# Row maxima of two heads in two 64-row tiles of the array, from the upper halves of the queries and keys

## The chip, the core and the metric

The kernel runs on one core of one Trainium2 chip. The core has a matrix engine (TensorE, here PE, its weight loads PEld), a vector engine (DVE), a scalar engine (ACT), GpSimd (POOL) and the queue of SyncE (SP), which issues the transfers. The metric is the device time of one execution in microseconds (us). Three executions took 2843.00, 2849.17 and 2850.83 us; the median is 2849.17.

## The reference

An image stack x of 4 x 128 x 32 x 32 goes through three layers: a non-local block, an attention layer over the 1024 tokens of each of 4 images, and a mixture of 8 experts, top 2. The change is in the attention layer. It has 16 heads of 64 (32 plain, 32 rotary) and three branches, each with its own keys and values:

```python
o1 = _attn(q, k1, v1, causal)            # all tokens, causal
o2 = _attn(q, ks, vs)                    # 256 selected tokens
o3 = _attn(q, kw, vw, winmask)           # causal, the last 64 tokens
o = g[:, 0] * o1 + g[:, 1] * o2 + g[:, 2] * o3
```

with `_attn` the softmax of `q k^T / 8` times v.

## The kernel before, in words

The program has three parts, one after the other: `heads_part` (non-local block, queries, keys and values of all heads, written to DRAM), `attention_part`, and `experts_part`. The attention part works by sides: a side is a pair of heads, so 8 sides to an image, 32 in all. `turns` is called three times: once to prepare the first side (OPENING), once as a loop over images 0 to 2 (MIDDLE), and once for image 3 (CLOSING).

Queries and keys are kept as an upper part (hi) and a rest (lo), in two sets of 128 rows. In the first set (q1a with k1a for branch 0, qa with kwa and ksa for branches 2 and 1) the upper 64 rows of a query tile are the hi parts of the head and the lower 64 its rests, and the keys have their hi parts twice, so that one matmul over 128 rows gives (hi + rest) of q times hi of k. The second set (q1b, qb, with k1b, kwb, ksb) adds hi of q times the rest of k, and in one row more the negated row maximum. The exponential thus comes straight out of PSUM.

In window w TensorE computes the exact pass of side w, and in between prepares side w+1, that is, finds the row maxima of its scores. The exact pass (`exact_pass`) has 25 units (branch, 512-column chunk of queries, 128-token tile of keys; 512 columns wide or fewer), each with `scores` (L1352, masks L1355 and L1358, L1360, for both heads), an exponential on ACT (L1409) and `products` (L1381, probabilities times values and, with a weight of ones, the sums; four column tiles of 32, fp32, in two passes). Two units' products follow every second unit's scores.

The preparation (`preparation`) is a list of fills, 43 to a side, in the order that TensorE, DVE and SP all follow: max2 (8 fills: head, pair of query tiles; the window), max1 (8; the selected), max0 (24; head, query tile, 512-column part; causal), three transposes ("rows") that turn the maxima into a row, and "whole", the last reduction of max0 (DVE). A fill of max0 is one matmul q1a x k1a (L1288), and where it reaches the diagonal a mask product with a bf16 identity (L1291). A fill of max1 has two products of 256 columns (L1299); one of max2 two of 192 (L1307), each with its mask (L1309). `window` spreads the list over the exact pass: after the scores of a unit it puts fills in until their share is that of the columns passed. Each fill takes one of three PSUM banks (SPARES) in turn; fill n waits until DVE has emptied fill n-3 (semaphore `emptied`), and DVE reduces each bank to its maxima (L1462, L1467).

SP issues the loads: `local` (qa, kwa, ksa and the second sets of branches 1 and 2; two sides ahead, L1206 to L1218), `whole` (q1a, k1a and the second set of branch 0; one side ahead, L1227 to L1232) and `row` (the maxima's row into row 64 of qb and q1b, L1239). Each transfer of queries fills 32 rows for both heads (`two`). `near`, `keys`, `far`, `late` count them.

Of the kernel before, what the change touches and what calls it, by code (L numbers as in the profile page):

```python
# [15 lines left out]
P = 128  # L16
B, C, T = 4, 128, 1024
NT = T // P
# [1040 lines left out]
class Plan:  # L1059


    def __init__(self, steps, sides, loads):
        self.steps, self.sides, self.loads = steps, sides, loads
        self.fills = self.of(("max0", "max1", "max2", "rows", "proj"))

    def of(self, kinds):
        return [x for x in self.steps if x[0] in kinds]

    def up_to(self, kind, side):

# [108 lines left out]
def turns(nc, m, plan, cur, nxt):  # L1179
# [7 lines left out]
                             "banks_free inverse_done divided o_done max_done")  # L1187
    negs = [m.small[:, k * HP * NT:(k + 1) * HP * NT] for k in range(3)]
    partial = m.small[:, 64:64 + HP * NT * 2].rearrange("p (h t a) -> p h t a", h=HP, t=NT)
    NEAR, KEYS, FAR, LATE = 8, 10, 5, 4  # L1190

    def two(x, side):

        return x[HP * NOPE * (side % 2):HP * NOPE * (side % 2 + 1)].rearrange("(h r) n -> r h n", h=HP)

    with nc.Block() as block:
        @block.sync
        def _(sp):
            def local(side):
                k, src = side % 2, cur if side < NSIDE else nxt  # L1200
                g, own = side % NSIDE // 2, side % NSIDE
                if side >= 2 and cur is not None:
                    sp.wait_ge(s["products_done"], len(UNITS) * (side - 2) + LOCAL)
                near, keys = s["near%d" % k], s["keys%d" % k]
                for at, comp in ((0, 2), (32, 4), (64, 3), (96, 5)):
                    sp.dma_start(m.qa[at:at + 32, k].bitcast(F32), two(src.q[g, comp], side)).then_inc(near, 16)  # L1206
                for at, comp in ((0, 0), (32, 2), (64, 0), (96, 2)):
                    sp.dma_start(m.kwa[at:at + 32, k].bitcast(F32), two(src.kw[g, comp], side)).then_inc(near, 16)
                for at, comp in ((0, 0), (32, 2), (64, 0), (96, 2)):
                    sp.dma_start(m.ksa[at:at + 32, k].bitcast(F32), two(src.ks[g, comp], side)).then_inc(keys, 16)  # L1210
                for at, comp in ((0, 2), (32, 4)):
                    sp.dma_start(m.qb[at:at + 32, k].bitcast(F32), two(src.q[g, comp], side)).then_inc(keys, 16)
                for at, comp in ((0, 1), (32, 3)):
                    sp.dma_start(m.kwb[at:at + 32, k].bitcast(F32), two(src.kw[g, comp], side)).then_inc(keys, 16)
                    sp.dma_start(m.ksb[at:at + 32, k].bitcast(F32), two(src.ks[g, comp], side)).then_inc(keys, 16)
                vv = slice(NW * own, NW * (own + 1))
                sp.dma_start(m.vw[:, k], src.vw[:, :, vv].rearrange("t p n -> p t n")).then_inc(s["late%d" % k], 16)
                sp.dma_start(m.vs[:, k], src.vs[:, :, vv].rearrange("t p n -> p t n")).then_inc(s["late%d" % k], 16)  # L1218

            def whole(side):  # L1220
# [5 lines left out]
                for at, comp in ((0, 0), (32, 4), (64, 1), (96, 5)):  # L1226
                    sp.dma_start(m.q1a[at:at + 32, k].bitcast(F32), two(src.q[g, comp], side)).then_inc(far, 16)  # L1227
# [42 lines left out]
        def _(pe):  # L1270
# [7 lines left out]

            def fill(n, kind, side, *a):

                if n >= SPARES:
                    pe.wait_ge(s["emptied"], n - SPARES + 1)
                bank, k = ps[:, 8 - SPARES + n % SPARES, :], side % 2
                if kind == "max0":
                    h, i, part = a
                    once("far%d" % k, 16 * FAR * plan.loaded("whole", side))
                    k0, k1 = part * CH, min((part + 1) * CH, (i + 1) * P)
                    mm = pe.matmul(bank[:, 0:k1 - k0], m.q1a[:, k, h, i * P:(i + 1) * P],  # L1288
                                   m.k1a[:, k, k0:k1], start=True, stop=True)
                    if k1 == (i + 1) * P:  # L1290
                        mm = pe.matmul(bank[:, k1 - k0 - P:k1 - k0], m.ident_bf[:], m.causal_q[:],  # L1291
                                       start=False, stop=True, skip_group_check=True)
                elif kind == "max1":
                    h, pair = a
                    once("near%d" % k, 16 * NEAR * plan.loaded("local", side))
                    once("keys%d" % k, 16 * KEYS * plan.loaded("local", side))
                    for i in range(2):
                        t = 2 * pair + i
                        mm = pe.matmul(bank[:, i * KEEP:(i + 1) * KEEP], m.qa[:, k, h, t * P:(t + 1) * P],  # L1299
                                       m.ksa[:, k, h, :], start=True, stop=True)  # L1300
                elif kind == "max2":
                    h, pair = a
                    once("near%d" % k, 16 * NEAR * plan.loaded("local", side))
                    for i in range(2):
                        t = 2 * pair + i
                        k0 = max(0, t * P - WINDOW)
                        pe.matmul(bank[:, i * KEEP:i * KEEP + WN], m.qa[:, k, h, t * P:(t + 1) * P],  # L1307
                                  m.kwa[:, k, h, k0:k0 + WN], start=True, stop=True, skip_group_check=True)
                        mm = pe.matmul(bank[:, i * KEEP:i * KEEP + WN], m.ident_bf[:],  # L1309
                                       m.window_q0[:] if t == 0 else m.window_q[:], start=False, stop=True,  # L1310
                                       skip_group_check=True)
                elif kind == "rows":
                    if a[0] == 0:
                        pe.wait_ge(s["max_done"], plan.nth(side) + 1)
                    else:
                        pe.wait_ge(s["emptied"], plan.up_to(("max1", "max2")[a[0] - 1], side))
                    mm = pe.transpose(bank[0:HP * NT, 0:P], negs[a[0]], m.ident[:])
                elif kind == "proj":
                    c, g = a[0], side // 2
                    cc = slice(c * CH, (c + 1) * CH)  # L1320
                    pe.wait_ge(s["divided"], plan.count("divide", side, SUMS.index((0, c)), PIECES - 1))
                    pe.wait_ge(s["o_done"], PIECES * (NC * g + c + 1))
                    pe.matmul(bank, m.wvp[:, g], m.products[:, 0, cc], start=True, stop=False)
                    mm = pe.matmul(bank, m.wproj[:, g], m.products[:, 1, cc], start=False, stop=True)
                mm.then_inc(s["fill_ready"], 1)

            def scores(side, u):
                br, c, j, q0, w = UNITS[u]
# [57 lines left out]
            for step in plan.steps:  # L1386
                if step[0] == "scores":
                    scores(*step[1:])
                elif step[0] == "products":
                    products(*step[1:])  # L1390
                elif step in plan.fills:
                    fill(n, *step)
                    n += 1

        @block.scalar
        def _(act):
# [41 lines left out]
        def _(dve):  # L1438
# [3 lines left out]
            for step in plan.steps:  # L1442
# [14 lines left out]
                n += 1  # L1457
                dve.wait_ge(s["fill_ready"], n)
                if kind == "max0":
                    _, _, h, i, part = step  # L1460
                    w = min((part + 1) * CH, (i + 1) * P) - part * CH
                    ins = dve.tensor_reduce(partial[:, h, i, part:part + 1], bank[:, 0:w], AX, ALU.max)  # L1462
                elif kind in ("max1", "max2"):
                    _, _, h, pair = step
                    w = KEEP if kind == "max1" else WN
                    at = h * NT + 2 * pair
                    ins = dve.tensor_reduce(negs[1 if kind == "max1" else 2][:, at:at + 2],  # L1467
                                            bank.rearrange("p (i n) -> p i n", i=2)[:, :, 0:w], AX, ALU.max,
                                            negate=True)
                elif kind == "rows":  # L1470

                    br = step[2]
                    if plan.nth(side) > 0:
# [560 lines left out]
```

## Time and profile before

The profiled execution took 2847.5 us, its span is 2845.7 us, the mean granted clock of TensorE 0.898 of full speed.

| engine | busy us | share of the span | instructions |
|---|---|---|---|
| PE | 2338.5 | 82% | 16656 |
| PEld | 1554.8 | 55% | 16656 |
| DVE | 1629.2 | 57% | 3043 |
| ACT | 1265.5 | 44% | 2777 |
| POOL | 669.0 | 24% | 687 |

```profile
PE   5586868663999999899999799999899999610995
PEclk9696979775999999999999899999899999755997
DMA  2254645477556555556556465665475461431113
```

The span is cut into 40 slices of 71 us; a digit is the busy share of a slice in tenths. Slices 10 to 34 are the attention part. PE's digits count a matmul from its start to its modelled end, and matmuls overlap, so a 9 does not say how many columns passed. PEclk is the granted clock of TensorE in tenths of full speed.

### The profile page before, as it was taken

What the parts mean: (1) busy time and instruction counts of PE and PEld (TensorE: products, weight loads), DVE (VectorE), ACT (ScalarE), POOL (GpSimd) and SP (SyncE); (2) the same over time, 40 slices, a digit from 0 to 9 for tenths busy, and PEclk for the clock granted to TensorE, in tenths of its full rate; (3) what the DMA queues carried; (4) which work ended last, traced back from release to release, by engine and by line L of the source; (5) the groups of instructions that cost most, each with busy time, mean ns of one, the idle gap of its engine ahead of it and who ended that gap; (6) DMA issues with size and microseconds to landing.
All of it is one profiled execution on the core that took longest, in us unless ns stands there. A gap on an engine that the chain in (4) does not pass through costs nothing. (4 is left out here: it accounts for less than half of the span.)

```text
span 2845.7 us, 46717 instructions
## 1 busy us (share of the span) xinstructions
PE 2338.5 (82%) x16656; PEld 1554.8 (55%) x16656; DVE 1629.2 (57%) x3043; ACT 1265.5 (44%) x2777; POOL 669.0 (24%) x687
## 2 busy tenths in 40 slices
PE   5586868663999999899999799999899999610995
PEld 3454545442666665566666466666566666410884
DVE  4757575724566556366466365565465664450666
ACT  2354545440555554455555345555355555410442
POOL 0264646581011001011011010010010110135332
PEclk9696979775999999999999899999899999755997
DMA  2254645477556555556556465665475461431113
GB/s 94 102 226 163 231 163 229 162 288 166 124 117 129 117 124 113 119 114 133 123 108 139 91 129 111 129 131 103 105 146 126 96 140 37 132 55 51 47 51 108
DMA packets 222862, 360.73 MB, mean 127 GB/s; under 512 B 68794, under 2 KB 124701, under 8 KB 222240
## 3 DMA queue, kind: packets, MB, share of 16 engines
q1 hardware_dynamic: 218304, 349.20, 49.2%
q0 software_dynamic: 4320, 8.43, 0.9%
q8 instruction: 140, 2.29, 0.4%
q14 instruction: 98, 0.80, 0.1%
HBM read 229.58 MB, written 126.56 MB: 125 GB/s over the span
## 5 line engine op out<-in xcount | busy, mean ns | idle before, releaser
L1409 ACT ACTIVATE prob<-ps 128x512 f32<-128x512 f32 (+5 forms) x1600 | 637.3, 442 | 732.8 <-PE ps L1360 586.8
L1462 DVE TENSOR_REDUCE maxima<-ps 128x1 f32<-128x512 f32 (+3 forms) x768 | 387.7, 548 | 294.8 <-PE ps L1288 147.0
L1432 POOL TENSOR_TENSOR products<-products,sums 128x256 f32<-128x256 f32 x192 | 140.4, 731 | 1605.9 <-DVE sums L1453 1604.6
L1381 PE MATMUL ps<-prob,plain 128*32 128x512 f32 (+5 forms) x3200 | 512.0, 443 | 0.0
L1467 DVE TENSOR_REDUCE maxima<-ps 128x2 f32<-128x512 f32 (+1 forms) x512 | 294.4, 608 | 243.2 <-PE ps L1309 108.5
L1453 DVE RECIPROCAL sums<-sums 128x256 f32<-128x256 f32 x192 | 331.5, 1736 | 104.1 <-ACT sums L1420 104.1
L1352 PE MATMUL ps<-q1a_s,k1a_s 128*128 128x512 f32 (+3 forms) x768 | 303.2, 395 | 0.0
L1360 PE MATMUL ps<-q1b_s,k1b_s 128*128 128x512 f32 (+3 forms) x768 | 301.2, 393 | 0.0
L1381 PE MATMUL ps<-prob,v_s 128*32 128x512 f32 (+3 forms) x1536 | 284.3, 491 | 0.0
L1288 PE MATMUL ps<-k1a_s,q1a_s 128*128 128x512 f32 (+3 forms) x768 | 234.7, 375 | 3.4 <-DMA k1a_s<-k1ah_dram 3.4
L1418 ACT ACTIVATE products<-ps,gates_a 64x512 f32<-64x512 f32 x192 | 131.0, 683 | 195.1 <-PE ps L1381 195.0
L1352 PEld LDWEIGHTS ps<-q1a_s,k1a_s 128*128 128x128 f32 x768 | 147.1, 191 | 126.8 <-issue 119.0
L953 POOL TENSOR_TENSOR pairs<-pairs 128x512 fp32r<-128x512 f32 (+1 forms) x112 | 134.7, 1208 | 290.6 <-ACT pairs L921 290.5
L1352 PE MATMUL ps<-qa_s,kwa_s 128*128 128x192 f32 (+2 forms) x576 | 175.0, 304 | 19.7 <-ACT prob L1409 16.1
L1360 PE MATMUL ps<-qb_s,kwb_s 128*128 128x192 f32 (+2 forms) x576 | 184.1, 322 | 0.0
L1352 PEld LDWEIGHTS ps<-qa_s,kwa_s 128*128 128x128 f32 x576 | 109.8, 191 | 98.3 <-issue 65.6
L1288 PEld LDWEIGHTS ps<-k1a_s,q1a_s 128*128 128x128 f32 x768 | 145.5, 196 | 21.8 <-DVE maxima L1462 8.4
L1360 PEld LDWEIGHTS ps<-q1b_s,k1b_s 128*128 128x128 f32 x768 | 151.3, 197 | 5.5
L1307 PE MATMUL ps<-kwa_s,qa_s 128*128 128x192 f32 x512 | 125.3, 327 | 34.7 <-DMA kwa_s<-kwh_dram 34.7
L1381 PEld LDWEIGHTS ps<-prob,plain 128*32 128x32 f32 x3200 | 147.2, 109 | 0.0
L1352 PE MATMUL ps<-qa_s,ksa_s 128*128 128x512 f32 x256 | 114.1, 446 | 37.4 <-issue 19.3
L1358 PE MATMUL ps<-window_k,ident_bf 128*128 128x192 bf16 (+2 forms) x576 | 141.3, 245 | 0.0
(333 smaller groups left out, 4862.7 us busy)
## 6 DMA issues: line engine op xcount, KB each, us to landing
qh_dram<-pairs SPq DMA_DIRECT2D x96, 512.0 KB, 2.7
kwh_dram<-pairs SPq DMA_DIRECT2D x64, 512.0 KB, 2.7
qa_s<-qh_dram SPq DMA_DIRECT2D x128, 256.0 KB, 4.4
kwa_s<-kwh_dram SPq DMA_DIRECT2D x128, 256.0 KB, 7.4
q1a_s<-qh_dram SPq DMA_DIRECT2D x128, 256.0 KB, 4.7
qb_s<-qh_dram SPq DMA_DIRECT2D x64, 256.0 KB, 9.1
kwb_s<-kwh_dram SPq DMA_DIRECT2D x64, 256.0 KB, 10.0
k1a_s<-k1ah_dram SPq DMA_DIRECT2D x32, 512.0 KB, 6.9
```

The costliest lines, as they stand in the source:

```text
L953: pool.tensor_tensor(lo.bitcast(F32R), lo, hi.bitcast(F32), ALU.subtract)\
L1288: mm = pe.matmul(bank[:, 0:k1 - k0], m.q1a[:, k, h, i * P:(i + 1) * P], m.k1a[:, k, k0:k1], start=True, stop=True)
L1352: pe.matmul(bank, kx, qx[:, k, h, q0:q0 + w], start=True, stop=False, skip_group_check=True)
L1358: pe.matmul(bank, m.ident_bf[:], m.window_k[:, at:at + w], start=False, stop=False, skip_group_check=True)
L1360: pe.matmul(bank, ky, qy[:, k, h, q0:q0 + w], start=False, stop=True, skip_group_check=True)\
L1381: mm = pe.matmul(ps[at:at + VD, SCORES + k % 2, q0 - c * CH:q0 - c * CH + w], w_, m.prob[:, n % PROBS, h, 0:w], start=first, stop=True, sk ...
L1409: act.activation(m.prob[:, u % PROBS, h, 0:w], ps[:, turn % SCORES, 0:w], ACT.Exp, scale=SCALE).then_inc(s["exp_done"], 1)
L1418: act.activation(m.products[rows, br, cc], ps[0:NW, SCORES + k % 2, :], ACT.Copy, scale=m.gates[0:NW, br:br + 1])
L1432: pool.tensor_tensor(o, o, m.sums[:, br, cc], ALU.mult).then_inc(s["divided"], 1)
L1453: dve.reciprocal(total, total).then_inc(s["inverse_done"], 1)
L1462: ins = dve.tensor_reduce(partial[:, h, i, part:part + 1], bank[:, 0:w], AX, ALU.max)
L1467: ins = dve.tensor_reduce(negs[1 if kind == "max1" else 2][:, at:at + 2], bank.rearrange("p (i n) -> p i n", i=2)[:, :, 0:w], AX, ALU.max, ...
```

## The change

Both heads of a side are prepared by one step. Its matmuls use 64 rows each: head 0 rows 0 to 63, head 1 rows 64 to 127, both with hi of q and hi of k only, into two banks. For that the loads put head 1's hi parts into the lower 64 rows of q1a and qa and its rests into the upper 64 (`upper_and_lower`); the exact pass still multiplies all 128 rows and gets the same sum. The masks stay products of 128 rows, after both heads' matmuls. 40 fills become 20 steps of two banks each; a step waits for both banks before its first matmul. DVE reduces the two banks one after the other, as before. Queries of the first sets come in 8 transfers of one head each instead of 4 of both.

```diff
 def preparation(side):
-    max0 = [("max0", side, h, i, part) for h in range(HP) for i in range(NT) for part in range(1 + (i >= NT // 2))]
-    max1, max2 = [[(kind, side, h, k) for h in range(HP) for k in range(NT // 2)] for kind in ("max1", "max2")]
-    todo = max2 + max1[:3] + [("rows", side, 2)] + max1[3:] + max0[:3] + [("rows", side, 1)] + max0[3:]
+    max0 = [("max0", side, i, part) for i in range(NT) for part in range(1 + (i >= NT // 2))]
+    max1, max2 = [[(kind, side, k) for k in range(NT // 2)] for kind in ("max1", "max2")]
+    todo = max2 + max1[:2] + [("rows", side, 2)] + max1[2:] + max0[:2] + [("rows", side, 1)] + max0[2:]
     return todo + [("whole", side, 0)]
...
-    NEAR, KEYS, FAR, LATE = 8, 10, 5, 4
+    NEAR, KEYS, FAR, LATE = 12, 10, 9, 4
+    def one(x, side, h):
+        return x[HP * NOPE * (side % 2) + NOPE * h:HP * NOPE * (side % 2) + NOPE * (h + 1)]
+    def upper_and_lower(first):
+        return [(h, at, comp + (lo ^ h)) for h in range(HP) for lo in range(2)
+                for at, comp in ((64 * lo, first), (64 * lo + 32, 4))]
...
-                for at, comp in ((0, 2), (32, 4), (64, 3), (96, 5)):
-                    sp.dma_start(m.qa[at:at + 32, k].bitcast(F32), two(src.q[g, comp], side)).then_inc(near, 16)
+                for h, at, comp in upper_and_lower(2):
+                    sp.dma_start(m.qa[at:at + 32, k, h].bitcast(F32), one(src.q[g, comp], side, h)).then_inc(near, 16)
...
+                def bank(h):
+                    if n + h >= SPARES:
+                        pe.wait_ge(s["emptied"], n + h - SPARES + 1)
+                    return ps[:, 8 - SPARES + (n + h) % SPARES, :]
+                upper = [slice(HD * h, HD * h + HD) for h in range(HP)]
                 if kind == "max0":
+                    both = [bank(h) for h in range(HP)]
+                    last = [pe.matmul(both[h][:, 0:k1 - k0], m.q1a[r, k, h, i * P:(i + 1) * P], m.k1a[r, k, k0:k1],
+                                      start=True, stop=True, skip_group_check=True) for h, r in enumerate(upper)]
                     if k1 == (i + 1) * P:
+                        last = [pe.matmul(both[h][:, k1 - k0 - P:k1 - k0], m.ident_bf[:], m.causal_q[:],
+                                          start=False, stop=True, skip_group_check=True) for h in range(HP)]
+                    for mm in last:
+                        mm.then_inc(s["fill_ready"], 1)
                 elif kind == "max1":
+                    both = [bank(h) for h in range(HP)]
                     for i in range(2):
+                        for h, r in enumerate(upper):
+                            mm = pe.matmul(both[h][:, i * KEEP:(i + 1) * KEEP], m.qa[r, k, h, t * P:(t + 1) * P],
+                                           m.ksa[r, k, h, :], start=True, stop=True, skip_group_check=True)
+                            if i == 1:
+                                mm.then_inc(s["fill_ready"], 1)
                 elif kind == "max2":
+                    both = [bank(h) for h in range(HP)]
                     for i in range(2):
+                        for h, r in enumerate(upper):
+                            pe.matmul(both[h][:, i * KEEP:i * KEEP + WN], m.qa[r, k, h, t * P:(t + 1) * P],
+                                      m.kwa[r, k, h, k0:k0 + WN], start=True, stop=True, skip_group_check=True)
+                    for h in range(HP):
+                        for i in range(2):
+                            mm = pe.matmul(both[h][:, i * KEEP:i * KEEP + WN], m.ident_bf[:],
+                                           m.window_q0[:] if 2 * a[0] + i == 0 else m.window_q[:], start=False, stop=True,
+                                           skip_group_check=True)
+                        mm.then_inc(s["fill_ready"], 1)
...
-                bank = ps[:, 8 - SPARES + n % SPARES, :]
+                for h in range(plan.banks(step)):
+                    bank = ps[:, 8 - SPARES + n % SPARES, :]
+                    n += 1
+                    dve.wait_ge(s["fill_ready"], n)
...
```

## Rows read from the trace of the kernel before

**Rows 1.** Busy time by stretch, us; two neighbouring windows of one side.

```profile
core 0: us, PE busy (x) PEld busy (x) DVE busy (x) ACT busy (x) POOL busy (x), PEclk, DMA share, GB/s
...
1468.64:1521.35 52.71, 51.33 (x430) 32.60 (x429) 26.45 (x47) 27.51 (x63) 1.45 (x2) 1.00 0.59 123
1521.35:1574.27 52.92, 51.02 (x425) 31.90 (x423) 38.12 (x54) 27.52 (x63) 10.26 (x14) 1.00 0.59 122
```

**Rows 2.** Waits in these two windows: total us, times, longest.

```profile
ACT prob L1409 <- PE ps L1360: 37.7, 37, 4.9
...
PEld ps L1323 <- DVE maxima L1467: 1.8, 1, 1.8
...
PE ps L1352 <- ACT prob L1409: 0.9, 3, 0.4
```

**Rows 3.** Timeline of PE, causal fills (start us, length us, instruction).

```profile
1507.45 0.37 PE L1288 MATMUL ps<-k1a_s,q1a_s 128*128 128x256 f32 x1
...
1507.70 0.42 PE L1288 MATMUL ps<-k1a_s,q1a_s 128*128 128x384 f32 x1
...
1508.00 0.47 PE L1352 MATMUL ps<-q1a_s,k1a_s 128*128 128x512 f32 x1
```

**Rows 4.** Timeline of PE, two products of a max2 fill.

```profile
1468.77 0.33 PE L1307 MATMUL ps<-kwa_s,qa_s 128*128 128x192 f32 x1
...
1468.98 0.33 PE L1307 MATMUL ps<-kwa_s,qa_s 128*128 128x192 f32 x1
```

**Rows 5.** Timeline of all engines, max1 fills and their reduction.

```profile
1481.29 0.45 PE L1299 MATMUL ps<-ksa_s,qa_s 128*128 128x256 f32 x2
...
1481.77 0.69 DVE L1467 TENSOR_REDUCE maxima<-ps 128x2 f32<-128x512 f32 x1 [1.26 <-PE ps L1299]
...
1482.49 0.63 PE L1299 MATMUL ps<-ksa_s,qa_s 128*128 128x256 f32 x4
```

**Rows 6.** Timeline of PE, from column tiles back to the full array.

```profile
1501.19 0.39 PE L1381 MATMUL ps<-prob,v_s 128*32 128x256 f32 x2
...
1501.40 0.39 PE L1381 MATMUL ps<-prob,v_s 128*32 128x256 f32 x2
1501.41 0.39 PE L1381 MATMUL ps<-prob,plain 128*32 128x256 f32 x2
1501.73 0.50 PE L1352 MATMUL ps<-q1a_s,k1a_s 128*128 128x512 f32 x1
1502.07 0.39 PE L1360 MATMUL ps<-q1b_s,k1b_s 128*128 128x512 f32 x1
1502.30 0.40 PE L1352 MATMUL ps<-q1a_s,k1a_s 128*128 128x512 f32 x1
```

**Rows 7.** Timeline of PE, first part: 64-row matmuls between 112-row ones.

```profile
207.15 0.39 PE L884 MATMUL ps<-cqs,wq_a 112*128 112x512 f32 x1
207.38 0.40 PE L885 MATMUL ps<-cqs,wq_b 112*128 112x512 f32 x1
207.71 1.12 PE L473 MATMUL ps<-arena,wo 64*128 64x512 f32 x2
208.76 0.50 PE L884 MATMUL ps<-cqs,wq_a 112*128 112x512 f32 x1
209.10 0.40 PE L885 MATMUL ps<-cqs,wq_b 112*128 112x512 f32 x1
```

**Rows 8.** Timeline of all engines, a masked 128-column fill, its reduction.

```profile
1499.48 0.23 PE L1291 MATMUL ps<-causal_q,ident_bf 128*128 128x128 bf16 x1
...
1499.74 0.29 DVE L1462 TENSOR_REDUCE maxima<-ps 128x1 f32<-128x128 f32 x1 [1.26 <-PE ps L1291]
```

**Rows 9.** Groups by shape in the first window, a reduction.

```profile
L1462 DVE TENSOR_REDUCE maxima<-ps 128x1 f32<-128x256 f32 x4 | 1.7, 422 | 3.9 <-PE ps L1291 3.9
```

**Rows 10.** Line L1206 in that window: ns min/median/max, first and last start.

```profile
L1206 SPq DMA_DIRECT2D qa_s<-qh_dram x4: 317/317/317, 1498.0 to 1499.5; - x4
```

**Rows 11.** Tile qb_s, 1495 to 1525 us: the maxima's rows, their reader.

```profile
L1360 PEld LDWEIGHTS ps<-qb_s,ksb_s x4: 187/190/192, 1520.4 to 1522.7; 128*128 128x128 f32 x4
...
L1239 SPq DMA_DIRECT2D qb_s<-mrows x2: 525/552/580, 1511.3 to 1511.9; - x2
...
DMA to landing us min/median/max: 7.6/8.6/10.0
```

More of the change, by code:

```diff
@@ L1063, in __init__, with banks @@
         self.steps, self.sides, self.loads = steps, sides, loads
-        self.fills = self.of(("max0", "max1", "max2", "rows", "proj"))
+        self.fills = [x for x in steps if x[0] in ("rows", "proj")
+                      or x[0] in ("max0", "max1", "max2") for h in range(self.banks(x))]
     def of(self, kinds):
         return [x for x in self.steps if x[0] in kinds]
+    def banks(self, step):
+        return HP if step[0] in ("max0", "max1", "max2") else 1
     def up_to(self, kind, side):
@@ L1225, in whole @@
                 far, late = s["far%d" % k], s["late%d" % k]
-                for at, comp in ((0, 0), (32, 4), (64, 1), (96, 5)):
-                    sp.dma_start(m.q1a[at:at + 32, k].bitcast(F32), two(src.q[g, comp], side)).then_inc(far, 16)
+                for h, at, comp in upper_and_lower(0):
+                    sp.dma_start(m.q1a[at:at + 32, k, h].bitcast(F32), one(src.q[g, comp], side, h)).then_inc(far, 16)
                 sp.dma_start(m.k1a[:, k].bitcast(F32), src.k1a).then_inc(far, 16)
@@ L1284, in fill @@
                 if kind == "max0":
-                    h, i, part = a
+                    i, part = a
                     once("far%d" % k, 16 * FAR * plan.loaded("whole", side))
                     k0, k1 = part * CH, min((part + 1) * CH, (i + 1) * P)
-                    mm = pe.matmul(bank[:, 0:k1 - k0], m.q1a[:, k, h, i * P:(i + 1) * P],
-                                   m.k1a[:, k, k0:k1], start=True, stop=True)
+                    both = [bank(h) for h in range(HP)]
+                    last = [pe.matmul(both[h][:, 0:k1 - k0], m.q1a[r, k, h, i * P:(i + 1) * P], m.k1a[r, k, k0:k1],
+                                      start=True, stop=True, skip_group_check=True) for h, r in enumerate(upper)]
@@ L1301, in fill @@
                 elif kind == "max2":
-                    h, pair = a
                     once("near%d" % k, 16 * NEAR * plan.loaded("local", side))
+                    both = [bank(h) for h in range(HP)]
                     for i in range(2):
-                        t = 2 * pair + i
+                        t = 2 * a[0] + i
                         k0 = max(0, t * P - WINDOW)
[L1307 to L1311, printed above, removed]
+                        for h, r in enumerate(upper):
+                            pe.matmul(both[h][:, i * KEEP:i * KEEP + WN], m.qa[r, k, h, t * P:(t + 1) * P],
+                                      m.kwa[r, k, h, k0:k0 + WN], start=True, stop=True, skip_group_check=True)
@@ L1322, in fill @@
                     pe.wait_ge(s["o_done"], PIECES * (NC * g + c + 1))
-                    pe.matmul(bank, m.wvp[:, g], m.products[:, 0, cc], start=True, stop=False)
-                    mm = pe.matmul(bank, m.wproj[:, g], m.products[:, 1, cc], start=False, stop=True)
-                mm.then_inc(s["fill_ready"], 1)
+                    room = bank(0)
+                    pe.matmul(room, m.wvp[:, g], m.products[:, 0, cc], start=True, stop=False)
+                    pe.matmul(room, m.wproj[:, g], m.products[:, 1, cc], start=False, stop=True)\
+                        .then_inc(s["fill_ready"], 1)
             def scores(side, u):
@@ L1392, in _ @@
                     fill(n, *step)
-                    n += 1
+                    n += plan.banks(step)
         @block.scalar
@@ L1455, in _ @@
                     continue
-                bank = ps[:, 8 - SPARES + n % SPARES, :]
[L1457 to L1470, printed above, removed]
+                for h in range(plan.banks(step)):
+                    bank = ps[:, 8 - SPARES + n % SPARES, :]
+                    n += 1
+                    dve.wait_ge(s["fill_ready"], n)
+                    if kind == "max0":
+                        _, _, i, part = step
+                        w = min((part + 1) * CH, (i + 1) * P) - part * CH
+                        dve.tensor_reduce(partial[:, h, i, part:part + 1], bank[:, 0:w], AX, ALU.max)\
+                            .then_inc(s["emptied"], 1)
+                    elif kind in ("max1", "max2"):
+                        w = KEEP if kind == "max1" else WN
+                        at = h * NT + 2 * step[2]
+                        dve.tensor_reduce(negs[1 if kind == "max1" else 2][:, at:at + 2],
+                                          bank.rearrange("p (i n) -> p i n", i=2)[:, :, 0:w], AX, ALU.max,
+                                          negate=True).then_inc(s["emptied"], 1)
+                if plan.banks(step) > 1:
+                    continue
+                if kind == "rows":
                     br = step[2]
```

13 lines of the change are left out of this document (3 added, 10 removed).

## The prediction

> **What bounds the kernel now.** I read the busy times by stretch first. The edited code runs in the attention part, from about 690 to 2405 us, as 32 preparations of a side (eight for each of four images). In two neighbouring windows, one with few reciprocals on DVE and one with many, the engine named PE is busy 51.3 of 52.7 us and 51.0 of 52.9 us at a granted clock of 1.00, while DVE goes from 26 to 38 us without moving the end, ACT has 27.5 and the DMA share is 0.59 [rows 1]. So a window lasts as long as TensorE's instruction stream. The waits say the same: over these two windows ACT waits 37.7 us for scores, PE waits 0.9 us for ACT, and the longest that a weight load waits for DVE's maxima is 1.8 us once, before a projection [rows 2]. Whatever is added to TensorE's stream in a window is therefore paid 32 times; what is taken off comes back 32 times, until something else is late.
>
> A busy PE is not yet a full PE, so I then read starts in the timeline, because the distance between two starts is the cost. A 256-column causal fill takes 0.25 us with its mask product (1507.45 to 1507.70) and a 384-column one 0.30 [rows 3]; that is 0.05 for each 128 columns, so about 0.20 at 128 and 0.35 at 512. A 192-column window product with its mask takes 0.21 [rows 4]. A 256-column product of max1 takes 0.12 (four in 0.63, of which the last one's tail is 0.28) [rows 5]. A 512-column one without mask takes 0.23 [rows 6].
>
> **What a change of tile shape costs.** This is what decides. The products of the probabilities run in 128-row by 32-column tiles. Two passes of 256 columns start 0.21 apart, but from the last pass to the next full-array matmul there are 0.33, so 0.12 passes in which nothing starts; and this first matmul takes 0.34 to the next, where the following takes 0.23, so 0.11 of its weight load is not hidden [rows 6]. That is the whole array and column tiles. Row tiles of 64 rows, which the change brings in, occur at one place in the trace, in the first part of the kernel (L473, alternating with 112-row matmuls that use the whole height). Going in, L885 to L473 is 0.33 instead of 0.23: 0.10. The two passes of L473, 512 columns each at the rate of rows 6 (256 in 0.21), should take 0.86 and take 1.05: 0.19, which is one exposed load and 0.08 of waiting on the way out. The first full-height matmul behind them takes 0.34 instead of 0.23, again 0.11 [rows 7]. So a change costs about 0.10 for emptying the array and 0.11 for a weight load that nothing covers: 0.21 in each direction. Into a mask product, whose bf16 load the trace never shows alone, the bounds are 0.10 (load free) and 0.21; I take 0.13, since next to fp32r loads its load is the shorter one (after a mask product starts, the next matmul follows in 0.04, rows 3).
>
> The Trainium skill has a rule against this change, in "TensorEngine Tiling (Array Packing)", Key Properties: a change of the tiling mode, not of the tile, drains the TensorE. It has no price; the rows above have one and agree with it.
>
> **The change, part by part, for one side.** The 24+8+8 single-head fills become 12 max0, 4 max1 and 4 max2 steps, each with both heads in two 64-row tiles. I take it that the two tiles stream at once. The rows show that only for column tiles (two of them start 0.01 apart at 1501.40 [rows 6]); for row tiles the bounds are full overlap and none, and none is a rival below. "TensorE: Matmul & The Clock Gate" in the Trainium skill (Part 3, the span model) has about 4 ns for each further tile, which no run here shows; by it the sum would be the same.
>
> The steps stand between scores and products by the same rule as before (share of the widths passed). Laid out over the 25 units, a step is preceded by full-array work nearly always: of 20 steps 19 change into row tiles, 12 go on to a mask in the full array, 3 go on to scores, and 5 go on to products or another step, where a change was paid before too or is not needed. (1) max2, four steps: before 4 x 0.21 = 0.86. After: 0.21 in, two overlapped pairs 0.24, 0.13 out to the masks, four mask products at 0.09 (0.21 less the 0.12 of a product): 0.94, a little more where scores follow. Together +0.4. (2) Masked max0, eight steps, each width from 128 to 512 twice. Before, both heads: 2 x (0.20+0.25+0.30+0.35) = 2.2 for four. After: one stream (0.05 for 128 columns, plus 0.02), masks 0.07 and 0.12: 0.26+0.31+0.37+0.42 = 1.36, plus 4 x (0.21+0.13) = 1.36: 2.72. Twice +0.52: +1.05. (3) Unmasked max0, four steps: before 0.46, after 0.21+0.23, and 0.21 more at the two with scores behind: +0.35. (4) max1, four steps: before 0.48, after 0.45, one exit of 0.21, one entry saved: -0.1. Sum +1.7 us a side. The switches are 19 x 0.21 + 12 x 0.13 + 3 x 0.21 = 6.2 us in it, and the work saved is 4.5.
>
> **The new wait.** A step asks for both of its banks before its first matmul, and there are three. A step right behind another one thus waits until DVE has emptied the first bank of the step before. In the layout this happens four times a side: max1 0 and 1, max0 tiles 0 and 1, tiles 3 and 4 (first part), tile 5 (second part) and 6. Behind the waiting weight load stands all of TensorE's queue. For max1 DVE starts 0.48 after the first matmul and takes 0.69 [rows 5], so the bank is free at 1.17, and TensorE is through with the step at 0.3: 0.85. For 128 columns DVE starts 0.26 after the mask product and takes 0.29 [rows 8]; in the new order the mask starts 0.3 after the first matmul, so free at 0.85, TensorE done at 0.45: 0.4. With 512 columns (0.69 in DVE) 0.75, with 256 (0.42 [rows 9]) 0.5. Sum 2.5, less 0.2 for emptying that passes meanwhile: 2.3. Bounds: 2.5, and 0 if time lost here is won back at waits for ACT; rows 2 has 0.9 us of such waits in two windows, so I stay near the upper end. Where a reciprocal stands ahead on DVE the wait can be longer, but in the present windows these 12 us on DVE move nothing.
>
> **Loads.** SP issues 8 more transfers a side (qa and q1a in eight pieces each instead of four), 0.5 us each (four in 1498.0 to 1499.5 by their starts [rows 10]), with the same bytes. Behind the 4 of them in `local` stands the maxima row of the next side: issued at 1511.3 and 1511.9, at least 7.6 us to land, needed at 1520.4 [rows 11]. That is a cover of about 1 us for 2 us more of issuing; but the landing is set by the bytes queued ahead, and the window gets 4 us longer. Cost 0; without both of these at most 1 x 32 = 32 us.
>
> **Sum.** 1.7 + 2.3 = 4.0 us a side, x 32 = 128. The profiled execution took 2847.5 (span 2845.7, 1.8 around it), so 2976; the median of the runs shown is 1.7 above that execution, which I leave in the range. DVE's and ACT's own work does not change.
>
> **Rivals.** (A) The switches cost as above, but the two-bank wait costs nothing: 1.7 x 32 = 54, 2902. For it: a pause of TensorE lets ACT run ahead. Against it: PE hardly waits for ACT now. (B) Faster: a change between the full array and row tiles is nearly free when both tiles are loaded at once, and L473's gaps are something of its own. Then 6.2 x 32 = 198 drop out: 4.5 saved, 2.3 lost, 2.2 x 32 = 70, 2778; without the two-bank wait too 2704. It decides below a third of the price, 0.07 instead of 0.21 for a change (6.2 f = 2.2). For it: that the row tiles seen come one at a time. Against it: three numbers at L473 that are those of the column tiles. (C) The two row tiles do not overlap: the 8192 columns a side taken out come back, 3.2 us at the 0.05 for 128 columns of rows 3 and some of it within the waits, say 3 x 32 = 96: 3072. (D) Part of the emptying passes in waits that exist anyway and the bank waits are short: within a few us of before, about 2855.
>
> **From this to the numbers.** Forecast 0.50, A 0.24, B 0.13 (all of it), C 0.05, D 0.08. The forecast's own range is 2945 to 3005. The range of 8 in 10 takes in A and most of D and leaves out B and C: 2852 to 3008. About 0.3% (8.5 us) is what measuring can tell from no change; with half of D inside it and a little faster: faster 0.14, same 0.05, slower 0.81.
>
> **What would show it.** In the profile after: L1360 or L1352 to the first matmul of a step about 0.33 instead of 0.23; both heads' starts 0.01 apart; a first weight load that waits for "DVE maxima" at the four places, 0.4 to 0.9 each; windows of about 56.8 us instead of 52.8. Windows under 52 us would prove me wrong, and so would starts without the 0.21, or a PEclk under 1.00, which my sum does not have.

## The result: 7.8% slower, and the profile after

The changed kernel takes 3067.15 us (median of 4, 3064.67 to 3076.65) against 2848.86 for the kernel before (median of 4): 1.0776 times as long, 95% interval 1.0748 to 1.0804. The direction was as predicted, the size was not: 218 us more, where 127 were forecast and 3008 us was the upper end. The profiled execution took 3076.65 us, span 3074.8.

From the page of the changed kernel, 40 slices, here of 77 us; the attention part is now slices 9 to 33:

```profile
PE   5686867638899897999998799989799999830796
PEclk9687888758999997999989889999899999955897
```

PE's digits are much as before. PEclk, which was 9 through the attention part but for an 8 at the ends of two images (slices 22 and 28) and its last slice, now has a 7 and five 8s in it. By stretch, one window with few reciprocals on DVE and two with many (columns as in [rows 1]):

```profile
1457.02:1513.52 56.50, 52.51 (x430) 29.76 (x429) 26.23 (x47) 27.75 (x63) 1.46 (x2) 1.00 0.50 114
1513.52:1581.80 68.28, 61.34 (x432) 33.40 (x431) 39.32 (x55) 27.79 (x63) 10.21 (x14) 0.85 0.44 95
1901.12:1962.24 61.12, 54.12 (x430) 30.07 (x429) 39.16 (x55) 27.55 (x63) 10.23 (x14) 0.97 0.49 106
```

The two kinds of window were alike before, 52.7 and 52.9 [rows 1]. Now an even window, with two reciprocals at its start, takes 56.5, the same to 0.03 us wherever it isn't the first of an image; the forecast for every window was 56.8. An odd window, with ten reciprocals in it, takes 61 to 68, and where it takes 68 the mean granted clock is 0.85. What the prediction missed is in the odd windows.

Timeline of PE in the changed kernel, a step of max2 between two units' scores:

```profile
1456.70 0.39 PE L1389 MATMUL ps<-qb_s,ksb_s 128*128 128x512 f32 x1
1457.02 0.47 PE L1332 MATMUL ps<-kwa_s,qa_s 64*128 64x192 f32 x4
1457.42 0.51 PE L1336 MATMUL ps<-window_q,ident_bf 128*128 128x192 bf16 x4
1457.71 0.47 PE L1381 MATMUL ps<-qa_s,ksa_s 128*128 128x512 f32 x1
```

The 0.32 us from L1389 to the first 64-row matmul, instead of 0.23, are what L473 showed [rows 7]. The four row-tile matmuls start in two pairs: the two heads of a pair 3 and 5 ns apart, the pairs 0.19 us.

The second of two steps standing together, timeline of PE:

```profile
1492.27 0.40 PE L1389 MATMUL ps<-q1b_s,k1b_s 128*128 128x512 f32 x1
1492.60 0.49 PE L1307 MATMUL ps<-k1a_s,q1a_s 64*128 64x512 f32 x2
1493.02 0.28 PE L1310 MATMUL ps<-causal_q,ident_bf 128*128 128x128 bf16 x2
1494.13 0.50 PE L1307 MATMUL ps<-k1a_s,q1a_s 64*128 64x512 f32 x2 [0.82 <-DVE maxima L1492]
1494.56 0.50 PE L1381 MATMUL ps<-q1a_s,k1a_s 128*128 128x512 f32 x1
```

From the second mask (1493.09) to the next step are 1.04 us, and the trace puts the wait down to DVE's maxima: TensorE waits for one bank. The same kind of place in an odd window, timeline of all engines:

```profile
1562.35 0.38 PE L1307 MATMUL ps<-k1a_s,q1a_s 64*128 64x256 f32 x2 [0.27 <-DVE maxima L1492]
...
1562.67 0.29 PE L1310 MATMUL ps<-causal_q,ident_bf 128*128 128x128 bf16 x2
1562.71 1.74 DVE L1482 RECIPROCAL sums<-sums 128x256 f32<-128x256 f32 x1
1564.38 0.69 DVE L1492 TENSOR_REDUCE maxima<-ps 128x1 f32<-128x256 f32 x2
...
1564.88 0.80 PE L1307 MATMUL ps<-k1a_s,q1a_s 64*128 64x512 f32 x2 [1.93 <-DVE maxima L1492]
```

The first line settles the overlap of the heads: from a pair of 256 columns to its mask are 0.32 us, from the pair of 512 above 0.42. So 256 more columns of both heads cost 0.10, which is the rate of a single stream in [rows 3]. The other lines show the wait. The reduction waited for stands behind a reciprocal, and the distance between the starts is 2.15 us. At another place of the window (max1, 1534.0) it is 1.84. After that one the clock falls; busy time by stretch around it:

```profile
1530.00:1536.88 6.88, 5.38 (x56) 2.90 (x54) 6.09 (x7) 2.87 (x9) 3.65 (x5) 1.00 0.00 0
1536.88:1550.50 13.62, 13.25 (x72) 7.56 (x69) 4.79 (x9) 4.66 (x10) 0.73 (x1) 0.50 0.07 22
```

For 13.6 us TensorE's granted clock is 0.50, 1.2 GHz instead of 2.4. Over the attention part (715 us to the last side's start) the clock's records sum to 212 us at half, against 58 before, and those 58 are at the ends of images.

### The profile page after: what moved, and what is told of

Same layout as the page of the kernel before. It is cut to its first block and busy times, and to the rows that moved or that the text cites. A ratio compares the mean times of both kernels' runs of the same rounds, so it can differ in the third digit from the quotient of the medians.

```text
span 3074.8 us, 47858 instructions
## 1 busy us (share of the span) xinstructions
PE 2428.1 (79%) x16656; PEld 1483.1 (48%) x16656; DVE 1637.0 (53%) x3043; ACT 1269.1 (41%) x2777; POOL 669.1 (22%) x687
## 5 line engine op out<-in xcount | busy, mean ns | idle before, releaser
L1410 PE MATMUL ps<-prob,plain 128*32 128x512 f32 (+5 forms) x3200 | 541.9, 464 | 0.0
L1381 PE MATMUL ps<-q1a_s,k1a_s 128*128 128x512 f32 (+3 forms) x768 | 312.0, 406 | 0.0
L1389 PE MATMUL ps<-q1b_s,k1b_s 128*128 128x512 f32 (+3 forms) x768 | 309.5, 404 | 0.0
L1410 PE MATMUL ps<-prob,v_s 128*32 128x512 f32 (+3 forms) x1536 | 303.9, 518 | 0.0
L1307 PE MATMUL ps<-k1a_s,q1a_s 64*128 64x512 f32 (+3 forms) x768 | 177.2, 453 | 88.1 <-DVE maxima L1492 87.2
L1381 PE MATMUL ps<-qa_s,kwa_s 128*128 128x192 f32 (+2 forms) x576 | 186.8, 324 | 31.2 <-ACT prob L1438 31.2
L1389 PE MATMUL ps<-qb_s,kwb_s 128*128 128x192 f32 (+2 forms) x576 | 190.2, 334 | 0.0
L1307 PEld LDWEIGHTS ps<-k1a_s,q1a_s 64*128 64x128 f32 x768 | 78.3, 192 | 182.4 <-DVE maxima L1492 128.2
L1389 PEld LDWEIGHTS ps<-q1b_s,k1b_s 128*128 128x128 f32 x768 | 155.9, 203 | 6.1
L920 ACT CAST pairs<-ps 128x512 fp32r<-128x512 f32 (+1 forms) x112 | 62.4, 557 | 158.5 <-PE ps L893 110.6
```

Of the source, the lines that this page charges most:

```text
L1307: last = [pe.matmul(both[h][:, 0:k1 - k0], m.q1a[r, k, h, i * P:(i + 1) * P], m.k1a[r, k, k0:k1], start=True, stop=True, skip_group_check= ...
L1381: pe.matmul(bank, kx, qx[:, k, h, q0:q0 + w], start=True, stop=False, skip_group_check=True)
L1389: pe.matmul(bank, ky, qy[:, k, h, q0:q0 + w], start=False, stop=True, skip_group_check=True)\
L1410: mm = pe.matmul(ps[at:at + VD, SCORES + k % 2, q0 - c * CH:q0 - c * CH + w], w_, m.prob[:, n % PROBS, h, 0:w], start=first, stop=True, sk ...
```

## The experiments

Ten kernels ran, each beside the kernel before on the same chip. All ratios are to the kernel before. The windows shown are two neighbours in the third image, an even and an odd one, in the columns of [rows 1].

**The reciprocals out of the way.**

```diff
-                    dve.reciprocal(total, total).then_inc(s["inverse_done"], 1)
+                    dve.reciprocal(total[:, 0:1], total[:, 0:1]).then_inc(s["inverse_done"], 1)
```

> The changed kernel, but each reciprocal on DVE covers one column instead of 256 (1.74 us becomes about 0.1); the other columns' sums are not inverted, so the result is not the reference's. Theory (the reciprocal ahead of the maxima makes TensorE wait at two steps standing together, and the granted clock falls behind the longest of these waits): windows with an odd number fall from 61 to 68 us to about 56.5, the length of the even ones; time at half clock in the attention part falls from 212 us to near the 58 of the kernel before; in all 2849 + 32 x 3.8 = 2971 (2960 to 2985). Rival 1 (64-row matmuls lower TensorE's activity and with it the clock, reciprocals or not): half-clock time stays near 200, 3020 to 3050. Rival 2 (odd windows are long for their projections and divisions' place in the order, not their length): no change, 3067.

2939.86 us, 1.0332 (1.0313 to 1.0351).

```profile
1759.55:1815.17 55.62, 52.36 (x432) 29.74 (x431) 23.34 (x47) 27.70 (x63) 1.45 (x2) 1.00 0.54 116
1815.17:1871.55 56.38, 52.55 (x430) 29.75 (x429) 24.16 (x55) 27.54 (x63) 10.12 (x14) 1.00 0.52 115
```

The odd windows lose 5 to 12 us and the low clock is gone (48 us at half in all). The 64-row matmuls are all still there, so rival 1, that they lower the clock by themselves, falls. It came out below my range, in part because even windows have a wait behind a reciprocal too, 0.9 us. Of the 218 us, 1.0776 - 1.0332 = 4.4%, about 126 us, hang on the length of the reciprocals. This kernel takes work off DVE as well (24 instead of 39 us in an odd window), so it doesn't tell length from load; the fourth and the eighth do.

**All rows, the same steps.** `m.q1a[r, ...]`, `m.k1a[r, ...]` and the like with `:` for `r`.

> The changed kernel, but the matmuls of the maxima use all 128 rows again (upper parts and rests); steps of two heads, two banks and the loads stay. This takes away only the changes of tile shape and the overlap of the two heads. Theory (of the 3.8 us that even windows gained, 1.7 are the shape and 2.1 the wait for two banks; clock falls after waits of about 2 us whatever the shape): even windows 54.8, odd ones still 58 to 65, half-clock time over 120 us, in all about 3000 (2970 to 3020). Rival 1 (64-row matmuls lower the clock): clock as in the kernel before (58 us at half), odd windows about 57, in all 2849 + 16 x 2.1 + 16 x 4 = 2947. Rival 2 (the shape costs nothing, all is the wait): even windows 56.5 or more, since the second head's columns come back: 3067 or more.

3044.77 us, 1.0705 (1.0683 to 1.0726).

```profile
1813.72:1869.47 55.75, 51.76 (x431) 32.94 (x430) 26.23 (x47) 27.65 (x63) 1.45 (x2) 1.00 0.53 116
1869.47:1932.04 62.57, 55.37 (x431) 34.28 (x429) 39.17 (x55) 27.56 (x63) 10.22 (x14) 0.95 0.47 103
```

Without any row tile the kernel is almost as slow, and its clock falls too: 144 us at half. So the loss is the steps of two banks, not the tiles. My split had 1.7 us of the even window for the tiles; this gives 0.75. The two long distances in an odd window are the same to 2 ns (1.835 and 2.146), and the clock falls behind 18 of the 30, for 92 us in all; with row tiles it falls behind 23 of the 30, for 150 us. The longest single stretch is 13.7 us in both, once here and four times there. So the 64-row matmuls do not start the low clock; that there is more of it with them rests on one trace of each.

**No step behind another.**

```diff
-            seen += UNITS[x[2]][4]
-            n = len(prepare) * seen // total
+            seen += 1
+            n = len(prepare) * seen // len(units_of)
```

> The changed kernel, but the preparation's 23 steps are spread by the number of units passed instead of their widths, so that no step stands right behind another. Row tiles and the switches all stay. Theory: the wait for the second bank goes: even windows 56.5 - 2.1 = 54.4; odd windows lose most of the wait behind a reciprocal too, about 55, and the clock stays at full: 2849 + 16 x 1.7 + 16 x 2.2 = 2911 (2895 to 2930). Rival 1 (the clock falls from 64-row matmuls): 2960 to 3000 with half-clock time near 200. Rival 2 (any step behind a reciprocal waits, together or not): even 54.4, odd windows 58 or more, over 2950. Rival 3 (the 3.8 us of even windows are all changes of shape): even windows 56.5, 2971 or more.

2997.72 us, 1.0531 (1.0508 to 1.0553).

```profile
1792.76:1846.20 53.44, 52.16 (x430) 29.63 (x429) 25.16 (x47) 27.50 (x63) 1.46 (x2) 1.00 0.56 120
1846.20:1908.50 62.30, 56.82 (x431) 32.23 (x430) 40.06 (x56) 27.66 (x63) 10.20 (x14) 0.92 0.48 104
```

Half right. Even windows come down to 53.4, 0.7 above the kernel before and 1.0 under what I expected. Odd ones do not: rival 2 was right there. A step of two banks behind a reciprocal waits though no step stands ahead of it (distances of 1.69 and 1.83), and the clock is at half for 225 us.

**And shorter reciprocals**, `PIECES = 4` for 2, on top of the spread list.

> As the spread kernel, and each sum is divided in four pieces of 128 columns instead of two of 256, so a reciprocal holds DVE about 0.9 us instead of 1.74. Theory: what waits behind reciprocals are left in odd windows halve: equal to the spread kernel or up to 1 us less for an odd window, 2895 to 2915. Rival (waits behind reciprocals are gone already): the same time; more where the additional issue costs on DVE and POOL show.

2878.03 us, 1.0111 (1.0090 to 1.0132).

```profile
1725.64:1779.06 53.42, 52.10 (x430) 29.64 (x429) 25.48 (x48) 27.45 (x63) 1.55 (x4) 1.00 0.56 120
1779.06:1832.94 53.88, 52.08 (x430) 29.66 (x429) 40.30 (x66) 27.44 (x63) 13.08 (x29) 1.00 0.54 120
```

That is under my range, which rested on the spread kernel taking 2911: instead of at most 1 us, 8 us of the odd window are gone, and the low clock with them. DVE has as much work as before (40.3 us against 40.1), in pieces of half the length. Not DVE's load but the longest piece of it was the cost.

**The row tiles' price by itself:** the same without them (the edits of the second and the fourth kernel together).

> As the kernel spread by units with divisions in four pieces (2878 us), but the maxima's matmuls use all 128 rows: no 64-row tiles, no overlap of the heads, all else alike. Theory (the shape changes cost more than the overlap saves, net 0.7 us a window, which is all that separates that kernel's windows from those of the kernel before): even windows 52.7, odd 53.2, in all 2856 (2846 to 2866). Rival 1 (the 0.7 are the other order or the two-bank steps): 2878. Rival 2 (by the terms of the prediction, shape net 1.7 a window): 2825.

2866.27 us, 1.0069 (1.0052 to 1.0085).

```profile
1712.44:1765.31 52.87, 51.50 (x430) 32.39 (x429) 25.50 (x48) 27.36 (x63) 1.66 (x4) 1.00 0.56 122
1765.31:1818.80 53.49, 51.57 (x430) 32.47 (x429) 40.09 (x66) 27.47 (x63) 13.03 (x29) 1.00 0.54 120
```

Just at the upper end of the theory's range. The change of shape costs 53.42 - 52.87 = 0.55 us and 53.88 - 53.49 = 0.39 a window net of what the overlap saves: 1.0111 - 1.0069, some 12 us in all. I had taken 54. (The first pair of kernels, with and without row tiles, is 1.0776 - 1.0705 apart, some 20 us, part of it through the clock.)

**Row tiles only where TensorE changes its shape anyway:** max1 and the unmasked steps of max0 as pairs just ahead of products; window and diagonal fills single and over all rows.

```diff
+SINGLES = {0: 2, 1: 2, 3: 2, 4: 1, 5: 1, 9: 1, 11: 1, 12: 1, 13: 2, 15: 1, 16: 2, 17: 2, 19: 2, 21: 2, 23: 2}
+PAIRED = (2, 6, 8, 10, 14, 18, 20, 22)
...
-PIECES = 2
+PIECES = 4
```

> Row tiles only where a step needs no mask (max1, and the first part of max0 for tiles 4 to 7), each put just before products, where TensorE changes its shape anyway; the window and diagonal fills are single-head fills over 128 rows as in the kernel before, in places between; divisions in four pieces. From the trace of the changed kernel: entry 0.09, a pair of 512 columns 0.42 to the products against 0.23 + 0.39 = 0.62 for two full ones, so 0.11 gained at each of four, and about 0.06 at each of four max1 steps: 0.7 a window. Theory: windows of 52.0, in all 2849 - 22 = 2827 (2815 to 2842). Rival 1 (the wait for two banks comes back at the fixed places): over 2860. Rival 2 (changes of shape eat the gain here too): 2845 to 2860.

**Its control**, the kernel before with `PIECES = 4` and nothing else.

> The kernel before with each sum divided in four pieces of 128 columns instead of two of 256. Control: since TensorE in the kernel before hardly waits for DVE, the length of a reciprocal should not matter: 2849 within 8 us. Rival (the long reciprocals cost the kernel before something too): 2820 to 2840; or the additional instructions cost: 2857 to 2870.

The mixed kernel took 2825.10 us, 0.9921 (0.9905 to 0.9937), as expected. The control took 2821.70, 0.9914 (0.9898 to 0.9930), which was not: some 25 us faster by one constant. The mixed kernel first, then the control:

```profile
1689.48:1741.73 52.25, 51.04 (x431) 31.17 (x429) 26.61 (x49) 27.48 (x63) 1.83 (x4) 1.00 0.56 123
1741.73:1793.72 51.99, 51.00 (x430) 31.16 (x429) 39.19 (x65) 27.53 (x63) 12.79 (x28) 1.00 0.56 124
```

```profile
1684.14:1736.17 52.03, 51.39 (x430) 32.60 (x429) 26.61 (x49) 27.49 (x63) 1.83 (x4) 1.00 0.61 124
1736.17:1788.22 52.05, 51.42 (x431) 32.59 (x429) 38.80 (x65) 27.49 (x63) 12.81 (x28) 1.00 0.58 124
```

So the shorter reciprocals alone give all that the mixed kernel gained, and its row tiles, two-bank steps and new order together bring nothing, where I had forecast 0.7 us a window; without the control I would have called the theory shown. The control is also faster than both kernels of this case. Both of its windows take 52.0, so 0.7 and 0.9 us a window came from reciprocals in the kernel before, and [rows 2] has a part of it: the weight load of a projection (L1323) waited 1.8 us for DVE. Kernel before, DVE and then PEld:

```profile
1473.17 1.74 DVE L1453 RECIPROCAL sums<-sums 128x256 f32<-128x256 f32 x1
1474.83 0.49 DVE L1467 TENSOR_REDUCE maxima<-ps 128x2 f32<-128x384 f32 x1
```

```profile
1475.78 0.30 PEld L1323 LDWEIGHTS ps<-products,wvp_g 128*128 128x128 f32 x2 [1.78 <-DVE maxima L1467]
```

The reduction it waits for stands behind a reciprocal there too. In the control the longest such wait is 0.8 us.

**Pairs with short reciprocals:** the changed kernel with `PIECES = 4`.

> The changed kernel with divisions in four pieces; steps still stand in pairs by the widths. Theory (the wait at the second of two steps is the time to empty a bank plus what stands ahead in DVE; the clock falls only after a long one): with reciprocals of 0.9 us even windows 56.0, odd ones 57.5, the clock as in the kernel before, in all 2849 + 16 x 3.3 + 16 x 4.8 = 2979 (2960 to 3000). Rival (the clock falls by how much waiting there is in all, not by the single long wait): half-clock time over 150 us, over 3010.

2965.68 us, 1.0417 (1.0396 to 1.0439).

```profile
1771.43:1827.84 56.41, 52.57 (x431) 29.76 (x430) 26.38 (x49) 27.58 (x63) 1.83 (x4) 1.00 0.51 114
1827.84:1884.61 56.77, 52.53 (x430) 29.73 (x429) 39.48 (x65) 27.56 (x63) 12.76 (x28) 1.00 0.53 114
```

As expected. No distance over 1.2 us is left in its windows, and 68 us are at half clock. Against the spread kernel with the same pieces it is 56.41 - 53.42 = 2.99 and 56.77 - 53.88 = 2.89 a window: that is the price of steps standing in pairs, with what else the order changes (I had 2.3).

**One wait by itself.** The kernel before, full array, old fills, and one added wait a window; and the same with 0.9 us more on DVE ahead of it (the last two lines of the diff are in the second kernel alone).

```diff
+                    if (h, i, part) == (1, NT // 2, 0):
+                        pe.wait_ge(s["emptied"], n)
...
+                    if (h, i, part) == (1, NT // 2 - 1, 0):
+                        dve.reciprocal(m.extra[:], m.extra[:])
```

> The kernel before, with one wait added a window and nothing else: at the second causal fill behind unit 20 (head 1, tile 4, first part) TensorE waits until all fills before it are emptied, full-array matmuls throughout. The wait should be the one seen at the second of two steps, a distance of 1.04 us from mask product to next matmul instead of 0.04. Theory (a wait of 1 us costs 1 us and leaves the clock alone): windows 53.7, half-clock time as in the kernel before, in all 2848 + 32 = 2880 (2870 to 2890). Rival (a wait on TensorE is partly won back at ACT): under 2865. Rival (any such wait lowers the clock): half-clock time over 120 us, over 2910.

> As the kernel with one added wait, and DVE has one more reciprocal of 128 scratch columns (0.9 us) ahead of the reduction waited for, so that the distance becomes 1.9 us. Theory (the granted clock falls behind single waits of that length, whatever the tile shape and however few they are): windows of 54.6 where it does not fall and several us more where it does, half-clock time 58 + 32 x 4 = 186 us or so (over 110), in all 2848 + 60 + 50 = 2958 (over 2925). Rival (the fall needs the many waits, or the 64-row matmuls, of the changed kernel): the clock as before, windows 54.6, 2908 (2898 to 2918).

2911.68 us, 1.0225 (1.0207 to 1.0244), and 2945.04, 1.0340 (1.0322 to 1.0359). Windows of the first and of the second:

```profile
1734.75:1788.51 53.76, 51.50 (x430) 32.66 (x429) 26.54 (x47) 27.55 (x63) 1.45 (x2) 1.00 0.58 120
1788.51:1844.99 56.48, 53.37 (x430) 33.24 (x429) 38.50 (x55) 27.47 (x63) 10.23 (x14) 0.97 0.55 114
```

```profile
1756.12:1812.32 56.20, 53.13 (x430) 32.97 (x429) 27.35 (x48) 27.58 (x63) 1.45 (x2) 0.97 0.55 115
1812.32:1869.69 57.37, 53.45 (x430) 33.24 (x429) 39.31 (x56) 27.49 (x63) 10.27 (x14) 0.97 0.53 113
```

In even windows the first was as expected: a distance of 1.11, window +1.05. In odd windows it was not, and the time left the range of 2870 to 2890. That is the finding in small. Timeline of PE, then of DVE, in the first kernel:

```profile
1366.13 0.23 PE L1293 MATMUL ps<-causal_q,ident_bf 128*128 128x128 bf16 x1
1368.83 0.77 PE L1290 MATMUL ps<-k1a_s,q1a_s 128*128 128x512 f32 x1 [2.47 <-DVE maxima L1464]
```

```profile
1366.39 1.74 DVE L1455 RECIPROCAL sums<-sums 128x256 f32<-128x256 f32 x1
1368.05 0.63 DVE L1464 TENSOR_REDUCE maxima<-ps 128x1 f32<-128x512 f32 x1
```

The wait was put where in odd windows a reciprocal stands ahead on DVE, so the same semaphore gives a distance of 2.70 instead of 1.11, and the clock falls behind it in some windows. I made in this experiment the very mistake of the prediction. The time at half clock is 78 us, so neither the theory (58) nor the rival of the clock (over 120) had it. The second kernel came within 13 us of its forecast by luck: in odd windows the distance is not 1.9 but 3.5 us, while the time at half clock is 109 us and not 186.

Here are all distances between matmul starts of 1.3 to 4 us that recur at one place of the windows, with how many of them had a low stretch beginning within 5 us of their start:

| distance, us | kernel | followed by low clock |
|---|---|---|
| 1.50 | the kernel before, and both with an added wait | 0 of 36 |
| 1.69 | spread | 6 of 15 |
| 1.83 | spread | 15 of 15 |
| 1.84 | changed | 11 of 15 |
| 1.84 | changed, all rows | 7 of 15 |
| 1.91 | added wait and reciprocal | 4 of 16 |
| 2.15 | changed | 12 of 15 |
| 2.15 | changed, all rows | 11 of 15 |
| 2.70 | added wait | 7 of 15 |
| 3.50 | added wait and reciprocal | 13 of 15 |

In the kernels that have none of them (short reciprocals, and all with four pieces) the low clock stands at the ends of images alone. The length of the wait does not decide by itself: 1.83 us in the spread kernel lowered the clock each time, 1.91 us in the full array one time in four. Where one wait stands alone a fall lasts 3.4 us and costs about 1.6 (54.57 and 56.20 in even windows of the second).

## Why the prediction was wrong

**The failed step** is in the part on the new wait: "Where a reciprocal stands ahead on DVE the wait can be longer, but in the present windows these 12 us on DVE move nothing." The observation, two windows 0.2 us apart, was nearly true, though it could not show what reciprocals cost both of them (0.7 and 0.9 us, by the control). The inference was false. In the kernel before a fill waits for the one three back, and even a DVE held for 1.74 us has mostly emptied that. A step of two banks waits for the fill just two back, so most of a reciprocal's length reaches TensorE: distances of 1.84 and 2.15 us. The first kernel shows it (4.4% gone with the reciprocals' length), the eighth confirms it with DVE's load unchanged (3.6% gone when they are halved), and the ninth shows it in the full array. My estimate of the waits alone: less what its low stretches can cost, an odd window would be 58.0 (68.27, 20.5 us at half) to 59.4 (61.12, 3.4 us at half), which is 1.6 to 3.0 over the 56.4 of the kernel with short reciprocals; even windows are 0.9 over theirs; times 16 that is 40 to 62 us.

**The second miss hangs on it:** the granted clock. The prediction named "a PEclk under 1.00, which my sum does not have" only as a sign of error. Half-clock time rose by 154 us over the kernel before, and is 164 us above the kernel with short reciprocals. At half clock the passes of the products with 512 columns start 0.85 us apart instead of 0.43 (changed kernel, 1565.6 and 1462.3 us), so low stretches cost at most half their length, 82 us; the 126 us of the first experiment less the waits above leave 64 to 82 for them.

**The two-bank wait** was right in mechanism and place (four a side, for "DVE maxima": distances of 1.15, 0.64, 1.04 and 0.77 us in the even window shown) and a little small: 2.3 forecast, 2.9 measured.

**The price of a change of shape** was right piece by piece: 0.32 to 0.33 into the row tiles, and 0.42 from a 512-column pair to its masks (about 0.2 of columns by [rows 3], the rest load and emptying), with the heads 3 to 5 ns apart. The sum over the steps was too high, 1.7 against 0.4 to 0.55 (0.75 in the first pair of kernels). I charged the first pair's load twice, in the entry of 0.21 and in the 0.12 of a load-bound product: the max2 step above takes 0.69 from its first matmul to the next scores, where before the same two fills took 0.77 (1468.64 to 1469.41; the sum had 4 x 0.21 = 0.86, which is 0.84). Timeline of PE, kernel before:

```profile
1468.64 0.25 PE L1307 MATMUL ps<-kwa_s,qa_s 128*128 128x192 f32 x1
...
1469.41 0.47 PE L1352 MATMUL ps<-qa_s,ksa_s 128*128 128x512 f32 x1
```

So with 0.09 of emptying the step costs about nothing, not 0.1.

**Even windows** came out at 3.8 against 4.0, which looks better than it is. With four pieces on both sides the parts are 2.99 for steps in pairs, 0.55 for the shape, and 0.84 (52.87 - 52.03) for two-bank steps in the order by units, which my sum does not have: 4.38 (56.41 - 52.03). A term too large, one too small, one missing, and a kernel before that paid 0.7 for its reciprocals gave the number by luck.

**The loads** cost nothing that shows: from 740 to 2400 us of the changed kernel's trace no wait of TensorE is put down to a transfer. **Rival C** (3072) met the time with a wrong reason: the heads do overlap. **Rivals A, B and D** fall with the even windows. The gap between shapes is there as forecast, but with 12 to 20 us out of 218 the change of shape was the least part. By the Trainium skill, "TensorEngine Tiling (Array Packing)", Key Properties, a change of the tiling mode drains TensorE; the trace agrees, with 0.09 us more before the first 64-row matmul.

What stays open: why low stretches in the windows last from 3.4 to 13.7 us, why the clock falls behind one wait and not behind a longer one, and what the 64-row matmuls have to do with it. The order by units with two-bank steps costs 1.0069 - 0.9914, some 44 us, against the control; I did not take that apart.

## What to carry to other kernels

When a change takes slack out of a ring of buffers, price the wait with the longest single instruction that can stand ahead on the engine that empties it, not with that engine's load: some 25 us came from splitting one instruction in two in a kernel whose DVE was busy 57% of the span. Look at odd and even, or first and last, repetitions of a window before you multiply one by the count. And give a change that touches two constants its control, or the gain goes to the wrong one.

## What the runs showed of the hardware

- Granted clock: with TensorE busy on both sides, distances between matmul starts of 1.69 to 3.5 us were followed by a stretch at 1.2 GHz in a quarter to all of the cases, by place and kernel; distances of 1.50 us in none of 36. In the kernels with an added wait the stretches were 3.4 us long but for one of 6.8, in the changed kernel up to 13.7.
- Two 64-row tiles of the array started their matmuls 3 to 5 ns apart and streamed together: both heads' pair and the way out to a mask took 0.32 us with 256 columns and 0.42 with 512.
- A 64-row matmul behind a full-array one started 0.09 to 0.10 us later than a full-array one would (0.32 to 0.33 for 0.23), and behind the way back the first full-array matmul took 0.34 instead of 0.23 to 0.24 to the next.
- A reciprocal of 256 columns took 1.74 us, one of 128 about 0.94; with twice as many of them DVE's busy time in an odd window stayed at 39 to 40 us.
